# V projected in transposed form, mostly during attention, and the FFN weights turned by DMA

## The reference, cut to what matters

```python
q = fq_sym(((layernorm(x) @ Wq + bq) / sqrt(32)), per row and head)
k, v = ctx @ Wkv + bkv                       # first and last 512 columns
k = fq_sym(k, per key and head)              # scale from 32 numbers
v = fq_sym(v, axis=keys)                     # one scale per column of V, over all 4096 keys
p = softmax(q @ k.T); p = round(p * 255 / max(p)) * max(p) / 255
x = x + tanh(g_xattn) * ((p @ v) @ Wp + bp)
w1, w2 = ternary(w1), ternary(w2)            # round(w / mean|w|) held to -1, 0, 1
h = layer_norm(gelu(silu(bitlinear(x, w1, b1))))
x = x + tanh(g_ffn) * bitlinear(h, w2, b2)
```

## Time and profile before

| what | value |
|---|---|
| median of 3 runs | 1906.11 us (1905.91 to 1906.17) |
| the profiled execution, its own time | 1901.73 us |
| its span | 1899.9 us |
| queries / keys and values / attention / finish, starts | 0 / 89.5 / 377.8 / 1596.3 us |
| PE busy | 1652.2 us (87%) |
| DVE busy | 1742.0 us (92%) |
| ACT busy | 1367.8 us (72%) |
| POOL busy | 1329.9 us (70%) |
| DMA | 240.75 MB, mean 127 GB/s |

### The profile page before, as it was taken

How to read it: one execution, slowest core, us unless ns; L and a number is a source line. 1 busy time by engine, 2 the same in 40 slices (tenths; PEclk the granted TensorE clock), 3 DMA queues, 4 the chain that set the end, 5 groups by cost and what they waited for, 6 DMA issues and landing times. The chain is left out here.

```text
span 1899.9 us, 36086 instructions
## 1 busy us (share of the span) xinstructions
PE 1652.2 (87%) x14056; PEld 820.5 (43%) x14072; DVE 1742.0 (92%) x2416; ACT 1367.8 (72%) x1315; POOL 1329.9 (70%) x1309
## 2 busy tenths in 40 slices
PE   8799999688888888888888888888888887678985
PEld 4345555334444444444444444444444444223331
DVE  7799999799999999999999999999999995478884
ACT  4434444378888888888888888888888884577772
POOL 0132222269999999999999999999999997335430
PEclk9899999869999999999999999999999998889997
DMA  6624444447756657766667666677565675022213
GB/s 217 234 75 142 142 153 137 127 99 130 156 118 145 141 119 148 131 138 140 133 136 144 119 145 149 121 147 130 131 145 129 140 144 138 13 54 69 73 39 78
DMA packets 641837, 240.75 MB, mean 127 GB/s; under 512 B 574265, under 2 KB 609145, under 8 KB 641410
## 3 DMA queue, kind: packets, MB, share of 16 engines
q1 hardware_dynamic: 640290, 235.51, 53.8%
q0 software_dynamic: 704, 1.62, 0.2%
q10 hardware_dynamic: 672, 1.31, 0.2%
HBM read 67.68 MB, written 27.30 MB: 50 GB/s over the span
## 5 line engine op out<-in xcount | busy, mean ns | idle before, releaser
L820 DVE TENSOR_SCALAR_CACHE_REDUCE att_scaled<-att_scores,layer_nsq 128x1536 f32<-128x1536 f32 (+1 forms) x768 | 1199.1, 1635 | 11.7 <-PE att_scores L792 11.4
L884 ACT ACTIVATE att_pairs<-att_scaled,att_bias_row 128x4096 uint8<-128x4096 f32 x256 | 950.3, 3712 | 184.1 <-POOL att_bias_row L832 163.1
L840 POOL CAST att_probsT<-att_pairsT 128x2048 bf16<-128x2048 uint8 x512 | 954.0, 1893 | 19.7 <-DMA att_pairsT<-att_pairs 5.5
L792 PE MATMUL att_scores<-first_k_head,first_q_head 96*128 96x512 bf16 x1024 | 295.6, 393 | 77.2 <-DVE att_scaled L820 66.0
L792 PE MATMUL att_scores<-att_k_head,att_q_head 96*128 96x512 bf16 x1024 | 286.3, 382 | 67.4 <-DVE att_scaled L820 63.4
L803 PEld LDWEIGHTS att_ps_o<-att_v_head,att_probsT 128*128 128x128 bf16 x8192 | 243.1, 96 | 61.9 <-issue 1.1
L803 PE MATMUL att_ps_o<-att_v_head,att_probsT 128*128 128x32 bf16 x8192 | 245.0, 176 | 0.6 <-POOL att_probsT L840 0.6
L779 PE MATMUL att_ps_o<-first_k_head,first_q_head 96*128 96x512 bf16 x768 | 209.5, 383 | 2.7 <-ACT layer_o_sum L876 2.6
L779 PE MATMUL att_ps_o<-att_k_head,att_q_head 96*128 96x512 bf16 x768 | 207.5, 379 | 0.0
L792 PEld LDWEIGHTS att_scores<-first_k_head,first_q_head 96*128 96x128 bf16 x1024 | 80.2, 99 | 223.2 <-DVE att_scaled L820 156.6
L792 PEld LDWEIGHTS att_scores<-att_k_head,att_q_head 96*128 96x128 bf16 x1024 | 79.0, 97 | 203.2 <-DVE att_scaled L820 146.4
(11 more groups left out here) (170 smaller groups left out, 1812.6 us busy)
## 6 DMA issues: line engine op xcount, KB each, us to landing
k_parts<-kv_k_stage SPq DMA_DIRECT2D x16, 768.0 KB, 4.7
q_w_in<-in_L_ffn_w_dram SPq DMA_DIRECT2D x32, 256.0 KB, 2.8
kv_weights_ctx_in<-in_ctx_dram SPq DMA_DIRECT2D x32, 256.0 KB, 4.6
kv_weights_w_in<-in_L_ffn_w_dram SPq DMA_DIRECT2D x32, 256.0 KB, 3.1
v_raws<-kv_v_stage SPq DMA_DIRECT2D x16, 512.0 KB, 4.4
att_v_raw<-v_raws SPq DMA_DIRECT2D x32, 256.0 KB, 2.9
att_k_head<-k_parts SPq DMA_DIRECT2D x96, 64.0 KB, 2.4
first_k_head<-k_parts SPq DMA_DIRECT2D x84, 64.0 KB, 2.5
```

Of the source, the lines that this page charges most:

```text
L792: last = pe.matmul(buffer[:, x:x + 512], q_head[slot][:, at:at + P], k_head[slot][:, STARTS[j] + x:STARTS[j] + x + 512], start=True, stop= ...
L820: dve.tensor_scalar(scaled[u][:, STARTS[j]:STARTS[j] + WIDTHS[j]], scores[(g * NCH + j) % 2][:, 0:WIDTHS[j]], kept["nsq"][:, g:g + 1], Non ...
L840: pool.tensor_copy(probsT[g % C_BUFS][:, parity * HALF:(parity + 1) * HALF, :].rearrange("p k q -> p (k q)"), turned.rearrange("p (n two) ...
L884: act.activation(pairs[g % R_BUFS][:, :].bitcast(U8).rearrange("p (c two) -> p two c", two=2), scaled[u][:, :].rearrange("p (two c) -> p t ...
```

## The change

V is computed transposed, so that a column of V is a partition. Its 512 columns are four groups of 128, each holding four heads. Group 0 is computed in the keys-and-values stage from blocks of 512 keys (one float32 matmul of 512 columns per key tile in place of four). Groups 1 to 3 are computed in attention: 96 matmuls of 512 columns, in the place of `keep_clock` at j = 0 of 96 units, from context chunks that were stored turned (`ctx_T`) and are loaded again by SP. `ps_o` becomes a single bank and the bank it frees holds V. ACT moves each block of 512 keys out of PSUM with the bias (`keep_values`), DVE takes the largest magnitude of the 4096 (`scale_group`), ACT rounds in quarters (`quantise_values`), and a DMA transpose brings each head's 32 x 4096 integers back to keys on partitions (`turn_values`). V lives in `w1T` and `w2T` meanwhile; the ternary weights are stored unturned in the keys-and-values stage (`terns`) and turned by 32 DMA transposes in units 190 to 252. POOL no longer touches V. The V half of Wkv is held in `wp`'s buffer.

```diff
@@ project_keys_values: SP
+                    m = g - 2
+                    if live(m, KT):
+                        sp.wait_ge(tern_ready, m + 1)
+                        sp.dma_start(t["terns"][m, :, :], tern[m % TERN_BUFS][:, :]).then_inc(tern_stored[m % TERN_BUFS], 16)
+
+                    j = (g - 5) // PER_BLOCK
+                    if g % PER_BLOCK == 1 and live(j, KEY_BLOCKS):
+                        sp.wait_ge(ctx_kept, PER_BLOCK * (j + 1))
+                        sp.dma_start(t["ctx_T"][j, :, :, :], inT[j % 2][:, :, :]).then_inc(ctx_stored[j % 2], 16)
...
-                sp.dma_start(t["v_raws"][part, :, i * GRP * D:(i + 1) * GRP * D].rearrange("h p k -> p h k"),
-                             v_stage[i % 2][:, part, :, :].rearrange("p h k d -> p h (k d)")).then_inc(v_stored[i % 2], 16)
@@ project_keys_values: PE
-                            last = pe.transpose(ps_w[s % 2][:, k, :], tern[s % 2][:, k * P:(k + 1) * P], kept["identb"][:, :])
-                            last = pe.matmul(ps_v[:, :], inT[r][:, k, :], wkv[:, k, C:2 * C], start=(k == 0), stop=(k == CT - 1))
...
+                    j, k = (g - 4) // PER_BLOCK, (g - 4) % PER_BLOCK
+                    if live(j, KEY_BLOCKS):
+                        if k == 0:
+                            pe.wait_ge(ctx_kept, PER_BLOCK * (j + 1))
+                            after(pe, v_kept, j)
+                        last = pe.matmul(ps_v[:, :], wv[:, k, 0:P], inT[j % 2][:, k, :], start=(k == 0), stop=(k == CT - 1))
@@ project_keys_values: ACT (copies to w1T and w2T removed; one of these per four tiles added)
+                    act.activation(values[:, j * BLOCK:(j + 1) * BLOCK], ps_v[:, :], ACT.Identity,
+                                   bias=kept["bv"][:, 0:1], scale=1.0).then_inc(v_kept, 1)
@@ project_keys_values: DVE
-                        dve.tensor_tensor(v_tile, heads(ps_v[:, :]), heads(bkv[:, C:2 * C]), ALU.add).then_inc(v_biased, 1)
-                        dve.tensor_tensor(heads(v_max[:, :]), v_tile, heads(v_max[:, :]), ALU.max).then_inc(kv_math, 1)
-                        dve.scalar_tensor_tensor(heads(v_low[:, :]), v_tile, -1.0, heads(v_low[:, :]), ALU.mult, ALU.max).then_inc(kv_math, 1)
+                    dve.tensor_reduce(v_mag[:, j:j + 1], values[:, j * BLOCK:(j + 1) * BLOCK], AX_X, ALU.max,
+                                      apply_absolute_value=True).then_inc(v_math, 1)
@@ attend: constants
+        GROUP_UNITS, GROUPS = 4 * QT, CT
+        BLOCK_UNITS, FIRST_CHUNK, LOAD_AHEAD = CT + 1, 4, 6
+        QUARTER = KEYS // 4
+        SCALE_AT, INTS_AT, TURN_AT = 46, 46, 9
+        W1_AT, W2_HIGH_AT, W2_LOW_AT = 190, 222, 238
+        def chunk_of(g):
+            n = g % GROUP_UNITS - FIRST_CHUNK
+            j, k = n // BLOCK_UNITS, n % BLOCK_UNITS
+            group = g // GROUP_UNITS + 1
+            return (group, j, k) if group < GROUPS and 0 <= j < KEY_BLOCKS and k < CT else None
@@ attend: SP
-                    sp.dma_start(v_raw[:, cols], t["v_raws"][h, :, cols]).then_inc(v_loaded, 16)
+                def load_chunk(group, j, k):
+                    n = chunk_index(group, j, k)
+                    after(sp, chunk_done, n - RING + 1)
+                    sp.dma_start(ctx_chunk[n % RING], t["ctx_T"][j, :, k, :]).then_inc(chunk_loaded[n % RING], 16)
+                def turn_values(h):
+                    sp.wait_ge(ints_ready, 4 * (h // 4 + 1))
+                    after(sp, pv_ready, (h - 1) * QT)
+                    sp.dma_start_transpose(v_head[h % 2][:, :].rearrange("p (k d) -> p k d", d=D),
+                                           value_ints[h % 4 * D:(h % 4 + 1) * D, :]).then_inc(v_turned[h % 2], 16)
+                def turn_weights(n, sem_of):
+                    j, i = n // 2 % 4, n // 8
+                    out = kept["w2T"][:, j * CT:(j + 1) * CT, i * P:(i + 1) * P] if n % 2 else kept["w1T"][:, :, n // 2 * P:(n // 2 + 1) * P]
+                    sp.dma_start_transpose(out, t["terns"][n, :, :]).then_inc(sem_of, 16)
@@ attend: PE
-                        if j == 0 and live(g - V_LAG, UNITS):
-                            after(pe, o_kept, g - V_LAG - 1)
-                            keep_clock(ps_o[r % 2], slot, at, 3)
+                        if j == 0 and live(g, UNITS) and chunk_of(g):
+                            value_chunk(*chunk_of(g))
+                        elif j == 0 and live(g - V_LAG, UNITS):
+                            after(pe, o_kept, g - V_LAG)
+                            keep_clock(ps_o, slot, at, 3)
...
                             pe.wait_ge(probs_ready, (g - V_LAG) * PIECES + PIECES)
+                            after(pe, o_kept, g - V_LAG)
...
                         if j == 2 and live(g - V_LAG, UNITS):
-                            after(pe, o_kept, g - V_LAG)
-                            keep_clock(ps_o[(r + 1) % 2], slot, at, 3)
+                            after(pe, o_kept, g - V_LAG + 1)
+                            keep_clock(ps_o, slot, at, 3)
@@ attend: DVE
+                def scale_group(group):
+                    dve.wait_ge(block_kept, block_index(group + 1, 0))
+                    dve.tensor_reduce(v_largest[:, :], values[:, :], AX_X, ALU.max,
+                                      apply_absolute_value=True).then_inc(scale_math, 1)
...
                 for g in range(UNITS):
+                    if g % GROUP_UNITS == SCALE_AT and g // GROUP_UNITS + 1 < GROUPS:
+                        scale_group(g // GROUP_UNITS + 1)
@@ attend: POOL
-                    pool.tensor_tensor(raw, raw, kept["v_inv"][:, h * D:(h + 1) * D].unsqueeze(1).to_broadcast([P, KT, D]),
-                                       ALU.mult).then_inc(v_scaled, 1)
@@ attend: ACT
+                    act.activation(values[:, cols], values[:, cols], ACT.Identity,
+                                   bias=round_up[:, 0:1], scale=kept["v_inv"][:, group:group + 1]).then_inc(v_upped, 1)
+                    act.wait_ge(v_upped, 4 * group + i + 1)
+                    act.activation(value_ints[:, cols], values[:, cols], ACT.Copy, bias=-ROUND).then_inc(ints_ready, 1)
...
                 for g in range(UNITS + O_LAG):
+                    if g < V_FIRST:
+                        quantise_values(0, 2 * g)
+                        quantise_values(0, 2 * g + 1)
+                    if chunk_of(g) and chunk_of(g)[2] == CT - 1:
+                        keep_values(*chunk_of(g)[0:2])
+                    i = (g % GROUP_UNITS - INTS_AT) // 2
+                    if g % 2 == 0 and 0 <= i < 4 and g // GROUP_UNITS + 1 < GROUPS:
+                        quantise_values(g // GROUP_UNITS + 1, i)
                     if live(g - O_LAG, UNITS):
                         r = g - O_LAG
                         act.wait_ge(pv_ready, r + 1)
-                                 ps_o[r % 2][:, 0:D]).then_inc(o_kept, 1)
+                                 ps_o[:, 0:D]).then_inc(o_kept, 1)
```

354 lines of the change are left out of this document (187 added, 167 removed).

## The result

The changed kernel takes 2264.36 us (median of 4 runs, 2258.07 to 2272.94) against 1906.01 (4 runs, 1904.25 to 1906.17) of the kernel before: ratio 1.189, 95% interval 1.187 to 1.191. The prediction was 2109, range 2035 to 2190. The direction and the wait were right, the size was not: the fall of PE's clock, rival B, whose chance I gave as 8%, came on top of the wait that I forecast.

A forecast was written before the change was run, and what follows sets the result against it. DVE was taken to bound attention, DVE and PE keys and values. From the profiled 1901.73 us, -70 (keys and values), +235 (wait loop) and +38 (work on it) gave 2105, with the median 4.4 higher 2109 us; range 2035 to 2190.

The forecast's parts named there:

- rival B: Attention: PE's clock falls to 1.2 GHz in half of the units, +173 us, so 2282 us; chance 8%.
- Keys and values: Keys-and-values stage: a key tile goes from 8.40 to 6.2 us, -70 us over 32 tiles; ends -60 and -84.
- POOL's two holds: Key tile: POOL's L608 and L606 hold DVE's L642 and L639; L642's 0.93 us can come back, two thirds kept.
- The loop: Attention: keep_clock at j = 2 waits for the copy of g - 5; 11.23 us per two units, +235 us.
- The clock: Attention: granted clock stays 1.00, as in 1740 to 1748 us at 72% busy; its fall was a rival at 8%.
- The work hanging on the loop: Attention: scale_group 12, quantise_values 19 and keep_values 7 us delay the loop, +38 us; ends 0 and +60.
- The other two new waits: Attention: PE's waits at j = 0 and PV for the copy of g - 6, a three-unit loop, 3.7 per unit: 0.
- The transfers: Attention: SP's added loads and transposes between pair transposes taken as hidden; upper end +48 us.
- my signs: DVE starts 5.6 us apart, idle 0.9 per unit; PE waiting at keep_clock; key tiles 6.2 us; clock 1.00.
- the sign that I had named as proof against me: Wrong if a granted clock below 1 appears past attention's start.
- Rival A: Attention: the wait at j = 2 doesn't bind, DVE stays the bound, only three scale_groups added: 1851 us; chance 8%.
- Rival C: Keys and values gain nothing, held by something unseen: 2179 us; chance 6%.

The follow-up runs named there:

- their run: Changed kernel with each of the 96 float32 value matmuls replaced by three bf16 ones, V of groups 1 to 3 not computed: 2234.06 us, ratio 1.173.
- the last versions: Changed kernel with all keep_clock matmuls written into the score buffer about to be filled: 1888.82 us; with reduce split, rounding spread and fewer keep_clock matmuls too: 1882.79 us.
- matmuls left out: Changed kernel without the three keep_clock matmuls at j = 2 and their wait: 1969.72 us, ratio 1.036.
- the matmuls moved: Changed kernel with the three keep_clock matmuls of j = 2 issued ahead of PV at j = 1: 1936.95 us, ratio 1.017.
- the fastest version: Changed kernel, keep_clock in the score buffer, reduce split in eight, rounding every third unit, two keep_clock matmuls at j = 2 in V units: 1882.79 us, ratio 0.988.
- gap filled: Kernel before, keep_clock at j = 2 waiting for the copy of g - 5, four unread matmuls to the other bank ahead of the wait: 2176.56 us, ratio 1.142.

## Why the prediction was wrong, by its steps

**Keys and values: right.** Tile 6.00 for my 6.2, gain 73.4 for 70. One of POOL's two holds moved to the instruction beside it, the other, of which I had kept two thirds, is gone. The Trainium skill ("SBUF — State Buffer", Who interferes with whom) says that only the port pair shared by DVE and GpSimd contends, as an exclusive lock; L645 above, which ends behind POOL's L615, agrees.

**The loop: right in place and size.** Predicted 5.62 per unit, measured 5.54 where the clock was full; the wait alone in the old kernel, with the clock nearly held, cost 271 us for my 235. The step from the copy to `keep_clock` that I had at 0.21 is 0.06.

**The clock: the step that failed.** I divided the loop by two ("DVE will be idle 0.94 per unit", in both parities) and then argued against rival B from a stretch where PE was 72% busy at 1.00. The mean was right and the evenness wrong: the idle time comes as 2.30 us in every other unit, and the granted clock went down to 0.81 on average. In the stretch that I leaned on, the longest wait of PE was 1.0 us. In the old kernel with the same wait the clock cost 119 us or more. In the changed one it is (6.01 - 5.54) x 250 = 118 by the units without V work, 6.01 being the mean of their three rows. I should have drawn two units of the loop out with PE's starts and ends and asked what the longest gap is, before comparing busy shares.

**The work hanging on the loop: too small.** Predicted 38 us. By the means of 16 units it is (6.51 - 6.01) x 192 = 96, 6.51 being the mean of the twelve rows of units 0 to 191. The single prices were right: the reduce 4.416 for my 4.5, rounding 1.229 and 1.056 for 1.04, `keep_values` 0.672 for 0.6; and so were reduce and rounding together, 31 predicted and 38 measured in units 44 to 53. The term that was mis-sized is that of units 4 to 43: 7 us for the moves and nothing for the float32 matmuls, where it is 61, of which the matmuls are some 30 by their run. I had counted them as hidden. That a loop at a falling clock has no slack to hide them in is my reading; the lower clock there is in the same 61 us. Then 5.54 - 4.68 = 0.86 x 250 = 215 for the loop, 118 and 96 make 429 of the measured 435. That sum is the stage's own time taken apart, so it proves none of the causes; the runs do.

**The other two new waits: "0" was wrong, though not visible.** I called the waits at j = 0 and at PV a loop over three units, 3.7 us each. It is a loop over two: exponential of g - 2, copy of g - 6, PV of g - 5, chunk 2 of g, exponential of g. It is masked by the wait at j = 2 in the changed kernel and shows when that one is gone, as gaps that lower the clock; taking the `keep_clock` matmuls out of it gave 1937 - 1889 = 48 us.

**The tail: not predicted, 9.6 us.** The last five units have no exponential left to wait for, but each PV still needs the copy before it, with six `keep_clock` matmuls between, at half clock. Kernel after, timeline:

```profile
1952.09 0.19 ACT L967 COPY layer_o_sum<-att_ps_o 128x32 f32<-128x32 f32 x1 [3.69 <-PE att_ps_o L874]
...
1952.33 2.74 PE L837 MATMUL att_ps_o<-first_k_head,first_q_head 96*128 96x512 bf16 x6 [0.28 <-ACT layer_o_sum L967]
...
1955.96 0.19 ACT L967 COPY layer_o_sum<-att_ps_o 128x32 f32<-128x32 f32 x1 [3.69 <-PE att_ps_o L874]
```

A unit of the tail is 3.87 us, and from the last unit's third chunk to the finish it is 23 us for 15 before.

**The transfers: right.** In the changed kernel ACT and POOL wait under 3 us in all for pair transposes; they land 0.6 us later, which shows only once the loop is gone.

**Of my signs**, the waits of PE at `keep_clock`, the tile and the transposes came as written. DVE waited 1.6 us per unit in place of 0.9, and the sign that I had named as proof against me, a granted clock below 1 in attention, is there. Rival A, without the wait, is near what the last versions show: 1883 for its 1851. Rival C didn't occur.

## What to carry to other kernels

Work that only keeps PE's clock up belongs in a place where it waits for nothing: in a PSUM buffer that the next matmul overwrites anyway, not in one whose reader is late. When a buffer loses its double, follow each wait that names it for two turns of the loop and write down the longest gap on PE, since the mean time per unit can be right and the clock still fall. A change whose time is lost to one such wait may be good in itself: this one is 0.8% faster than the kernel before with its `keep_clock` matmuls in another buffer, and 1.2% with its delays spread as well.

## What the runs showed of the hardware

- PE at 79% of busy time was granted 0.81 (kernel after) and 0.85 (matmuls left out) on average; at 85% it was granted 0.95 with the matmuls moved and 0.99 in the fastest version, and at 88% 0.97 (gap filled); 72% in eight microseconds of the finish ran at 1.00. So a mean share of busy time didn't tell the clock here. It fell behind gaps of 2.30 us in every second unit, though not behind each of them; it held with single gaps of 1.1 us in every unit and fell behind 1.11 and 0.93 us shortly after each other. That fits idle time that counts by how it is grouped, but no run changed the grouping and left the amount of matmul work as it was. The Trainium skill ("TensorE: Matmul & The Clock Gate", A second HAM failure mode: psum-queue depth-cycling) describes a clock that goes back and forth when PE idles briefly and often between groups of matmuls; the traces agree in kind, and I gave too little for it.
- Four matmuls per unit that nobody reads made a kernel 119 us faster (2295 to 2177), and three fewer per unit made one 33 us slower (1937 to 1970), with the clock at 0.97 for 0.84 and at 0.85 for 0.95.
- The least landing of a pair transpose rose from 3.6 us to 4.2 in the versions with the change, whether the chunk loads or the addresses were as before or not, and that of the unchanged finish stage from 3.7 to 4.4; with only the wait changed in the old kernel they stayed 3.6 and 3.7.
